# A product moved from VectorE to GpSimd and a reciprocal cut in two, in the attention of a perceiver layer

## The chip, the cores and the metric

The kernel is one program on one core of a Trainium2 chip. The metric is the device time of one execution in microseconds (us), as the median of three runs. A core has four computing engines that work side by side, each in the order of its own instructions: TensorE (PE in the rows) multiplies matrices, VectorE (DVE) and ScalarE (ACT) work on tiles in SBUF and PSUM, and GpSimd (POOL) works on tiles in SBUF. SyncE (SP) issues the transfers. The engines wait for one another through counting semaphores.

## The reference

The layer is a cross-attention of 512 tokens to 8192 context rows with 16 heads of 32 columns and a small MLP, then a local attention, then a feed-forward with quantized weights. The change touches the cross-attention alone:

```python
q = (x @ Wq + bq).reshape(B, N, NUM_HEADS, HEAD_DIM)
k = (y @ Wk + bk).reshape(B, M, NUM_HEADS, HEAD_DIM)
v = (y @ Wv + bv).reshape(B, M, NUM_HEADS, HEAD_DIM)
scores = jnp.einsum('bnhd,bmhd->bhnm', q, k) * scale
attn = jax.nn.softmax(scores, axis=-1)
out = jnp.einsum('bhnm,bmhd->bnhd', attn, v).reshape(B, N, IMAGE_DIM)
```

## The kernel before

The attention runs head by head (`h = 2 * i + s`, 16 heads), and in a head block by block: 16 blocks `q` (QUADS) of 512 keys. The softmax needs the largest score of each row before the exponentials, so two computations run interleaved. For the present head the scores are computed with the keys on the partitions (`scores`, L1120), four tiles to a block, and ScalarE takes their exponentials (L1337). For a head that comes two blocks less than one head later, the scores are computed a first time with the tokens on the partitions (`pre`, L1080), four tiles to a block, and VectorE takes the row maximum of each (`tile_max`, L1380). Those first scores stand in three PSUM banks (PRE_BANKS), so a `pre` tile can't start before the maximum of the tile three places earlier is taken. TILE_ORDER is 0, 3, 1, 2. Tile 3 (SUM_J) is read twice: after its maximum ScalarE overwrites it with exponentials and sums them (`sum_tile`, L1293). The numbers that come out of this, one for each block, are `part_sum`.

TensorE's order in a block is PE_ORDER: score 0, pre tile 0, score 1, pre tile 3, a denominator step, score 2, pre tiles 1 and 2, score 3. Behind them comes the product of the exponentials with the values (`weighted`, L1133), for the block before.

The denominators of the softmax are collected in three ways: GpSimd adds three of a block's four tiles of exponentials for 384 tokens (`add_up`, L1525 and L1529); TensorE sums the fourth (L1144) and at the end what GpSimd added (`denominator`, L1160); and for the last 128 tokens the sums come from `part_sum`. These have to be weighted first. ScalarE computes the 16 weights after block 1 (`weigh`, L1301), VectorE multiplies them with `part_sum` (L1392) and adds the 16 products (L1394) at block 3 (`take_share`), ScalarE spreads the result on a diagonal after block 3 (`spread_share`, L1308), and TensorE adds it to the denominators in block 5 (`add_share`, L1169). Each of these steps counts up `share_steps` by one.

The head before is finished inside the next one: `denominator` at the end of block 1, the reciprocal of 128 columns in PSUM by VectorE ahead of block 2's maxima (`invert`, L1398), `output` on TensorE at the end of block 5 (L1178), and `scale_out` on VectorE ahead of block 6's maxima (L1405). Nothing is scheduled at run time: all orders are those of the code. In the last head no first scores are left to compute.

Of the kernel before, what the change touches and what calls it, by code (L numbers as in the profile page):

```python
# [22 lines left out]
ALU = mybir.AluOpType  # L23
# [7 lines left out]
P = 128  # L31
# [7 lines left out]
H = 16  # L39
# [43 lines left out]
class Chain:  # L83
# [14 lines left out]
    def wait(self):  # L98
        self.eng.wait_ge(self.sem, self.n + self.moving)
# [35 lines left out]
def perceiver(nc, a, out):  # L135

    with ExitStack() as whole:
# [75 lines left out]
        part_sum = piece([2, QUADS])  # L213
        part_share = piece([QUADS])
# [35 lines left out]
        def of_block(ap, c):  # L250

            return ap.rearrange("p (j c r) -> p c j r", c=P // HD, r=HD)[:, c]
# [632 lines left out]
        with ExitStack() as st:  # L885
# [14 lines left out]
            recip = sb("recip", [P, P])  # L900
# [7 lines left out]
            den_ps = banks[:, DEN_BANK]  # L908
# [4 lines left out]
            share_steps = sem("share_steps")  # L913
# [7 lines left out]
            recip_ready = sem("recip_ready")  # L921
# [20 lines left out]
            LASTPAIR = H // 2 - 1  # L942
# [26 lines left out]
            def ahead(q, last):  # L969

                return last >= (1 if q < QUADS - AHEAD else 2)

            WEIGH_AT, SHARE_AT, SHARE_ADD_AT = 1, 3, 5
            LAST_SUMMED = QUADS - 2

            def summed_tiles(h, q):

                if not (isinstance(h, int) and h == H - 1):
                    return POOL_TILES
                return DVE_TILES if q < LAST_SUMMED else 0  # L980
# [9 lines left out]
            def quad_no(i, s, q):  # L990

                return 2 * QUADS * i + QUADS * s + q
# [82 lines left out]
            def _(pe):  # L1075
# [61 lines left out]
                def add_to_denominator(i, s, q):  # L1137

                    h = 2 * i + s
                    if q == 0:  # L1140
                        wait(pe, recip_ready, h)
                    for n in range(summed_tiles(h, q), BT):
                        for t in range(TT):
                            last = nc.tensor.matmul(den_ps[t * HD:(t + 1) * HD, 0:P - HD], ones[:],  # L1144
                                                    of_block(prob[:, q % PSLOTS, n, 0:ADDED], t),
                                                    start=q == 0 and n == summed_tiles(h, q), stop=False)
                    last.then_inc(den_added, 1)
# [24 lines left out]
                def output(i, s, bank):  # L1172

                    h = 2 * i + s
                    pe.wait_ge(recip_ready, h + 1)
                    pe.wait_ge(pv_read, h + 1)
                    for t in range(TT):
                        last = nc.tensor.matmul(pre_ps[t * HD:(t + 1) * HD, bank, 0:P], fold[:],  # L1178
                                                of_block(pv_sum[:, s], t), start=True, stop=True)
                    last.then_inc(o_ready, 1)  # L1180
# [81 lines left out]
                for m in range(EARLY_M):  # L1262
                    hidden(m, range(DK - 1, DK))
                pe.wait_ge(pv_read, H)
                pe.wait_ge(recip_ready, H)
                pe.wait_ge(o_scaled, H)
                for m in range(EARLY_M, FM):
                    hidden(m, range(DK))
                for t in range(TT):
                    pe.wait_ge(h_whole, t + 1)  # L1270
                    for k in range(FM):
# [3 lines left out]
                        for p, (sh, sw) in enumerate(PRODUCTS):  # L1275
                            last = nc.tensor.matmul(banks[:, y_bank[t]], hT_halves[:, sh, k, t * P:(t + 1) * P],
                                                    w2_halves[:, k // 2, sw, k % 2 * D:(k % 2 + 1) * D],
                                                    start=k == 0 and p == 0, stop=k == FM - 1 and p == 2)
# [97 lines left out]
            def _(dve):  # L1376
                def tile_max(s, part, j, tile, bank):

                    dve.wait_ge(pre_ready, tile + 1)
                    nc.vector.tensor_reduce(tile_low[:, s, j, part:part + 1], pre_ps[:, bank], AX.X, ALU.max,  # L1380
                                            negate=True).then_inc(pre_read, 1)

                def head_max(h, s):

                    dve.wait_ge(pre_read, TILES * h - TT * AHEAD)
                    wait(dve, row_ready, h - 1)
                    nc.vector.tensor_reduce(neg_max[:, s], tile_low[:, s], AX.X, ALU.min).then_inc(max_ready, 1)

                def take_share(h, s):

                    dve.wait_ge(share_steps, 4 * h + 1)
                    nc.vector.tensor_tensor(part_share[:], part_share[:], part_sum[:, s], ALU.mult).then_inc(share_steps, 1)  # L1392
                    dve.wait_ge(share_steps, 4 * h + 2)
                    nc.vector.tensor_reduce(share[:], part_share[:], AX.X, ALU.add).then_inc(share_steps, 1)  # L1394

                def invert(i, s):
                    dve.wait_ge(den_ready, 2 * i + s + 1)
                    nc.vector.reciprocal(recip[:], den_ps[:, 0:P]).then_inc(recip_ready, 1)  # L1398

                def scale_out(i, s, bank):  # L1400
                    h = 2 * i + s
                    dve.wait_ge(recip_ready, h + 1)
                    dve.wait_ge(o_ready, h + 1)
                    wait(dve, o_stored[s], 16 * TT * i)
                    nc.vector.tensor_tensor(o_out[:, s], pre_ps[:, bank, 0:P], recip[:], ALU.mult).then_inc(o_scaled, 1)  # L1405
# [35 lines left out]
                def out_low(k):  # L1441

                    dve.wait_ge(o_high, k + 1)
                    nc.vector.scalar_tensor_tensor(out=oT_halves[:, 1, k], in0=oT[:, k], scalar=bv[:, k:k + 1],
                                                   in1=oT_halves[:, 0, k], op0=ALU.add, op1=ALU.subtract).then_inc(o_low, 1)
# [14 lines left out]
                def head(i, s, first, last):  # L1460
                    h = 2 * i + s
                    before = (i, 0) if s else (i - 1, 1)
                    for q in range(QUADS):
                        if q == 2 and not first:
                            invert(*before)
                        if q == OUTPUT_AT + 1 and not first:
                            scale_out(*before, out_bank)
                        if q == SHARE_AT:
                            take_share(h, s)
                        if ahead(q, last):  # L1470
                            s_of, part = (1 - s, q + AHEAD) if q < QUADS - AHEAD else (s, q + AHEAD - QUADS)
                            for n, j in enumerate(TILE_ORDER):
                                tile_max(s_of, part, j, TILES * h + TT * q + n,
                                         turn_of[(q, j)] % PRE_BANKS)
                        if q == QUADS - AHEAD - 1 and last >= 1:
                            head_max(h + 1, 1 - s)
                        if last == 0:
                            if q < LAST_SUMMED:
                                sum_tiles(q)
                            if q in SPLIT_AT:  # L1480
                                split_weights(SPLIT_AT.index(q))
                            if q in O_LOW_AT:
                                out_low(O_LOW_AT.index(q))
# [5 lines left out]
                    head(i, 1, False, 2)  # L1489
                head(LASTPAIR, 0, False, 1)  # L1490
                head(LASTPAIR, 1, False, 0)
                invert(LASTPAIR, 1)
                scale_out(LASTPAIR, 1, out_bank)
                split_weights(len(SPLIT_AT))
                out_low(DK - 1)
# [18 lines left out]
            @block.gpsimd  # L1514
            def _(pool):

                def add_up(i, s, q):
                    Q = quad_no(i, s, q)
                    sums = sum_pool[:, s]
                    if q:  # L1520
                        pool.wait_ge(p_ready, BT * Q + POOL_TILES)
                    if q == 1:

                        wait(pool, den_ready, 2 * i + s - 1)
                        nc.gpsimd.tensor_tensor(sums, prob[:, 0, 0:POOL_TILES, 0:ADDED], prob[:, 1, 0:POOL_TILES, 0:ADDED],  # L1525
                                                ALU.add).then_inc(pool_summed, 2)
                    elif q > 1:
                        pool.wait_ge(pool_summed, Q)
                        nc.gpsimd.tensor_tensor(sums, sums, prob[:, q % PSLOTS, 0:POOL_TILES, 0:ADDED],  # L1529
                                                ALU.add).then_inc(pool_summed, 1)  # L1530

                for s in range(2):
                    for q in range(QUADS):
                        add_up(0, s, q)
                for i in range(1, LASTPAIR):
                    for s in range(2):
                        for q in range(QUADS):
                            add_up(i, s, q)
                for q in range(QUADS):
                    add_up(LASTPAIR, 0, q)  # L1540

        xattn.close()

# [510 lines left out]
        with ExitStack() as st:  # L2054
# [8 lines left out]
            h = sb("h", [P, 512])  # L2063
# [332 lines left out]
```

## Time and profile before

| | |
|---|---|
| median of 3 runs | 1363.45 us (1362.64 to 1365.55) |
| the profiled execution, its own time | 1362.23 us |
| its span in the trace | 1360.4 us |
| the attention, from the first scores to the last denominators | about 343 to 1093 us of the span |
| one head in the middle | 47.3 us |
| granted TensorE clock in the attention | 1.00 |

PE is busy 95% of the span, DVE 82%, ACT 72%, POOL 52%. These are averages over stages of different kinds. Inside a head all four engines are busy over 80% of the time, so what counts there is which one makes another wait, and that is read from the timeline of one head. A row of the timeline is a start in us, a duration in us, the engine, the line, what is written and read, the shape and the number of merged instructions. In square brackets stands the time for which the engine was idle before, with what ended it.

### The profile page before, as it was taken

What the parts mean: (1) busy time and instruction counts of PE and PEld (TensorE: products, weight loads), DVE (VectorE), ACT (ScalarE), POOL (GpSimd) and SP (SyncE); (2) the same over time, 40 slices, a digit from 0 to 9 for tenths busy, and PEclk for the clock granted to TensorE, in tenths of its full rate; (3) what the DMA queues carried; (4) which work ended last, traced back from release to release, by engine and by line L of the source; (5) the groups of instructions that cost most, each with busy time, mean ns of one, the idle gap of its engine ahead of it and who ended that gap; (6) DMA issues with size and microseconds to landing.
All of it is one profiled execution on the core that took longest, in us unless ns stands there. A gap on an engine that the chain in (4) does not pass through costs nothing. (4 is left out here: it accounts for less than half of the span.)

```text
span 1360.4 us, 39341 instructions
## 1 busy us (share of the span) xinstructions
PE 1297.9 (95%) x16386; PEld 665.6 (49%) x16386; DVE 1118.7 (82%) x1819; ACT 976.4 (72%) x2002; POOL 708.3 (52%) x320
## 2 busy tenths in 40 slices
PE   7999999999899999999999999999999999999998
PEld 4444444444345444544544454454444445566454
DVE  5768888888898988898888988889887745678895
ACT  4454555544899999999999999999999931354332
POOL 0321221222688878978887888888789001111121
PEclk9999999999999999999999999999999999999999
DMA  7667777876452212122211212221211030492000
GB/s 262 188 167 203 214 228 209 226 215 171 136 170 63 64 59 70 39 70 67 53 57 57 69 40 70 69 69 40 67 59 32 4 148 1 108 212 32 1 9 24
DMA packets 127798, 137.49 MB, mean 101 GB/s; under 512 B 44995, under 2 KB 108995, under 8 KB 125699
## 3 DMA queue, kind: packets, MB, share of 16 engines
q1 hardware_dynamic: 127622, 134.98, 35.2%
q8 instruction: 130, 2.13, 0.7%
q14 instruction: 46, 0.38, 0.1%
HBM read 75.70 MB, written 44.17 MB: 88 GB/s over the span
## 5 line engine op out<-in xcount | busy, mean ns | idle before, releaser
L1380 DVE TENSOR_REDUCE early<-attend_banks 128x1 f32<-128x512 f32 x952 | 590.2, 682 | 64.0 <-PE attend_banks L1080 62.6
L1529 POOL TENSOR_TENSOR early<-early,attend_prob 128x1152 f32<-128x1152 f32 x210 | 556.4, 2650 | 65.6 <-ACT attend_prob L1337 46.1
L1337 ACT ACTIVATE attend_prob<-attend_banks 128x512 f32<-128x512 f32 x1024 | 554.4, 601 | 16.5 <-PE attend_banks L1120 9.0
L1120 PE MATMUL attend_banks<-early,k_first 97*32 97x512 f16 x2560 | 265.5, 380 | 2.9 <-ACT attend_prob L1337 1.6
L1080 PE MATMUL attend_banks<-k_first,early 96*32 96x512 f16 x2272 | 215.8, 380 | 9.0 <-DVE early L1380 7.7
L1293 ACT ACTIVATE attend_banks<-attend_banks,early 128x512 f32<-128x512 f32 x238 | 160.0, 672 | 18.3 <-DVE early L1380 18.3
L1120 PE MATMUL attend_banks<-early,attend_k_rest 97*32 97x512 f16 x1536 | 162.0, 380 | 1.1 <-ACT attend_prob L1337 0.9
L1080 PE MATMUL attend_banks<-attend_k_rest,early 96*32 96x512 f16 x1536 | 143.4, 380 | 8.9 <-DVE early L1380 8.9
L1133 PE MATMUL attend_banks<-attend_prob,attend_vh_odd 128*32 128x512 f32 x1024 | 135.6, 592 | 0.0
L1133 PE MATMUL attend_banks<-attend_prob,wkv_area 128*32 128x512 f32 x1024 | 135.6, 592 | 0.0
L1080 PEld LDWEIGHTS attend_banks<-k_first,early 96*32 96x32 f16 x2272 | 74.8, 95 | 113.9 <-DVE early L1380 91.8
L513 POOL TENSOR_TENSOR project_w_whole<-project_grid,project_qscale 128x704 f32<-128x704 f32 x24 | 33.3, 1386 | 172.6 <-DVE project_grid L667 172.6
L1120 PEld LDWEIGHTS attend_banks<-early,k_first 97*32 97x32 f16 x2560 | 82.7, 95 | 47.4 <-ACT attend_prob L1337 30.3
L567 ACT ACTIVATE project_v<-project_v_ps 128x512 f32<-128x512 f32 x64 | 38.1, 597 | 84.7 <-PE project_v_ps L806 84.7
L1144 PE MATMUL attend_banks<-attend_prob,ones 128*32 128x96 f32 x2208 | 96.0, 245 | 0.0
L1144 PEld LDWEIGHTS attend_banks<-attend_prob,ones 128*32 128x32 f32 x2208 | 75.6, 110 | 34.6 <-issue 1.2
L1080 PEld LDWEIGHTS attend_banks<-attend_k_rest,early 96*32 96x32 f16 x1536 | 48.1, 95 | 81.9 <-DVE early L1380 68.8
L507 POOL TENSOR_TENSOR project_qn<-early,project_qinv 128x704 f32<-128x704 f32 x24 | 38.0, 1583 | 88.0 <-issue 50.2
L549 ACT ACTIVATE early<-project_k_ps,project_bk 128x512 f32<-128x512 f32 x64 | 44.0, 687 | 54.0 <-PE project_k_ps L787 52.0
L804 PE MATMUL project_v_ps<-project_w_hi,project_yT_hi 128*128 128x512 f16 x192 | 73.8, 384 | 5.7 <-ACT project_v L567 5.7
L787 PE MATMUL project_k_ps<-project_yT_hi,project_w_hi 128*128 128x512 f16 x192 | 72.5, 379 | 2.3 <-ACT project_q_hi L603 1.4
L805 PE MATMUL project_v_ps<-project_w_lo,project_yT_hi 128*128 128x512 f16 x192 | 73.7, 384 | 0.0
(230 smaller groups left out, 1997.0 us busy)
## 6 DMA issues: line engine op xcount, KB each, us to landing
v_scratch<-project_v SPq DMA_DIRECT2D x16, 1024.0 KB, 8.9
early<-in_ctx_dram SPq DMA_DIRECT2D x16, 768.0 KB, 6.2
k_first<-k_scratch SPq DMA_DIRECT2D x36, 256.0 KB, 3.4
k_scratch<-project_k_hi SPq DMA_DIRECT2D x64, 128.0 KB, 3.0
k_scratch<-project_k_lo SPq DMA_DIRECT2D x64, 128.0 KB, 3.1
attend_vh_odd<-v_scratch SPq DMA_DIRECT2D x8, 1024.0 KB, 5.1
wkv_area<-v_scratch SPq DMA_DIRECT2D x7, 1024.0 KB, 5.0
attend_k_rest<-k_scratch SPq DMA_DIRECT2D x24, 256.0 KB, 3.4
```

The source lines that it names most:

```text
L549: nc.scalar.activation(kf[:, g % 2], k_ps[:, g % 2], ACT.Identity, bias=bk[:, g:g + 1], scale=1.0 / WSCALE).then_inc(kf_ready, 1)
L787: last = nc.tensor.matmul(k_ps[:, g % 2], (w_lo if p == 2 else w_hi)[:, 0, k, cols], (yT_lo if p == 1 else yT_hi)[:, u, k], start=(k, p) = ...
L804: nc.tensor.matmul(v_ps[:, t % 2], yT_hi[:, u, k, cols], w_hi[:, 1, k], start=k == 0, stop=False)
L805: nc.tensor.matmul(v_ps[:, t % 2], yT_hi[:, u, k, cols], w_lo[:, 1, k], start=False, stop=False)
L1080: last = nc.tensor.matmul(pre_ps[c * HD:(c + 1) * HD, bank, :], q_stack[0:KROWS, h, queries], keys_at(s, part * BLK, (part + 1) * BLK)[0:K ...
L1120: last = nc.tensor.matmul(s_ps[c * HD:(c + 1) * HD, s_bank(h, n), :], key_rows[:, c * HD:(c + 1) * HD], q_stack[0:KROWS + 1, h, :], start= ...
L1133: last = nc.tensor.matmul(pv_ps[t * HD:(t + 1) * HD, :], vh[s][:, BT * q + t, :], prob[:, q % PSLOTS, t, :], start=q == 0, stop=q == QUADS ...
L1144: last = nc.tensor.matmul(den_ps[t * HD:(t + 1) * HD, 0:P - HD], ones[:], of_block(prob[:, q % PSLOTS, n, 0:ADDED], t), start=q == 0 and n ...
L1293: nc.scalar.activation(pre_ps[:, bank], pre_ps[:, bank], ACT.Exp, bias=tile_low[:, s, SUM_J, part:part + 1], accum_out=part_sum[:, s, part ...
L1337: nc.scalar.activation(prob[:, q % PSLOTS, t, :], s_ps[:, s_bank(h, BT * q + t)], ACT.Exp).then_inc(p_ready, 1)
L1380: nc.vector.tensor_reduce(tile_low[:, s, j, part:part + 1], pre_ps[:, bank], AX.X, ALU.max, negate=True).then_inc(pre_read, 1)
L1529: nc.gpsimd.tensor_tensor(sums, sums, prob[:, q % PSLOTS, 0:POOL_TILES, 0:ADDED], ALU.add).then_inc(pool_summed, 1)
```

## The change

`take_share` loses its multiplication. GpSimd does it (`multiply`), behind its addition for block 2, and the steps that follow move one block later: the sum of the products on VectorE to block 4, `spread_share` to the end of block 4, and `add_share` to block 6. `invert` now takes 64 of the 128 columns; the first half stands ahead of block 2's first maximum and the second half ahead of its third. `recip_ready` counts two for each head.

```diff
-            WEIGH_AT, SHARE_AT, SHARE_ADD_AT = 1, 3, 5
+            INVERT_AT = 2
+            WEIGH_AT, MULTIPLY_AT, SHARE_AT, SHARE_ADD_AT = 1, 2, 4, 6
...
                 def take_share(h, s):
 
-                    dve.wait_ge(share_steps, 4 * h + 1)
-                    nc.vector.tensor_tensor(part_share[:], part_share[:], part_sum[:, s], ALU.mult).then_inc(share_steps, 1)
                     dve.wait_ge(share_steps, 4 * h + 2)
                     nc.vector.tensor_reduce(share[:], part_share[:], AX.X, ALU.add).then_inc(share_steps, 1)
 
-                def invert(i, s):
+                def invert(i, s, half):
+
+                    cols = slice(half * P // 2, (half + 1) * P // 2)
                     dve.wait_ge(den_ready, 2 * i + s + 1)
-                    nc.vector.reciprocal(recip[:], den_ps[:, 0:P]).then_inc(recip_ready, 1)
+                    nc.vector.reciprocal(recip[:, cols], den_ps[:, cols]).then_inc(recip_ready, 1)
...
                     for q in range(QUADS):
-                        if q == 2 and not first:
-                            invert(*before)
...
+                        if not first and q == INVERT_AT and not ahead(q, last):
+                            for half in range(2):
+                                invert(*before, half)
                         if ahead(q, last):
...
                             for n, j in enumerate(TILE_ORDER):
+                                if not first and q == INVERT_AT and n % 2 == 0:
+                                    invert(*before, n // 2)
                                 tile_max(s_of, part, j, TILES * h + TT * q + n,
...
+                def multiply(h, s):
+
+                    pool.wait_ge(share_steps, 4 * h + 1)
+                    nc.gpsimd.tensor_tensor(part_share[:], part_share[:], part_sum[:, s], ALU.mult).then_inc(share_steps, 1)
+
...
                         nc.gpsimd.tensor_tensor(sums, sums, prob[:, q % PSLOTS, 0:POOL_TILES, 0:ADDED],
                                                 ALU.add).then_inc(pool_summed, 1)
+                    if q == MULTIPLY_AT:
+                        multiply(2 * i + s, s)
```

The other hunks double the value of each wait on `recip_ready`, cut the last head's reciprocal in two as well, and give GpSimd the product of the last head.

VectorE, from the last blocks of one head to the last of the next. Before: the maxima (L1380), the whole reciprocal ahead of block 2's four, then product and sum (L1392, L1394).

```order
L1380 TENSOR_REDUCE early<-attend_banks 128x1 x16
L1398 RECIPROCAL attend_recip<-attend_banks 128x128
L1380 TENSOR_REDUCE early<-attend_banks 128x1 x4
L1392 TENSOR_TENSOR early<-early 128x16
L1394 TENSOR_REDUCE early<-early 128x1
L1380 TENSOR_REDUCE early<-attend_banks 128x1 x12
L1405 TENSOR_TENSOR attend_o_out<-attend_banks,attend_recip 128x128
L1380 TENSOR_REDUCE early<-attend_banks 128x1 x32
```

The same place after the change, with lines one higher:

```order
L1381 TENSOR_REDUCE early<-attend_banks 128x1 x16
L1399 RECIPROCAL attend_recip<-attend_banks 128x64
L1381 TENSOR_REDUCE early<-attend_banks 128x1 x2
L1399 RECIPROCAL attend_recip<-attend_banks 128x64
L1381 TENSOR_REDUCE early<-attend_banks 128x1 x6
L1393 TENSOR_REDUCE early<-early 128x1
L1381 TENSOR_REDUCE early<-attend_banks 128x1 x8
L1406 TENSOR_TENSOR attend_o_out<-attend_banks,attend_recip 128x128
L1381 TENSOR_REDUCE early<-attend_banks 128x1 x32
```

Two maxima now stand between the halves of the reciprocal. The product is gone, and the sum (L1393) stands ahead of block 4's maxima, six maxima behind the second half.

ScalarE, from `weigh` (L1301) in block 1 over `spread_share` (L1308). Before:

```order
L1301 ACTIVATE early<-early 128x16
L1337 ACTIVATE attend_prob<-attend_banks 128x512 x3
L1293 ACTIVATE attend_banks,early<-attend_banks,early 128x512
L1337 ACTIVATE attend_prob<-attend_banks 128x512 x4
L1293 ACTIVATE attend_banks,early<-attend_banks,early 128x512
L1337 ACTIVATE attend_prob<-attend_banks 128x512
L1308 ACTIVATE early<-ident,early 128x128
L1337 ACTIVATE attend_prob<-attend_banks 128x512 x3
```

After the change:

```order
L1302 ACTIVATE early<-early 128x16
L1338 ACTIVATE attend_prob<-attend_banks 128x512 x3
L1294 ACTIVATE attend_banks,early<-attend_banks,early 128x512
L1338 ACTIVATE attend_prob<-attend_banks 128x512 x4
L1294 ACTIVATE attend_banks,early<-attend_banks,early 128x512
L1338 ACTIVATE attend_prob<-attend_banks 128x512 x4
L1294 ACTIVATE attend_banks,early<-attend_banks,early 128x512
L1338 ACTIVATE attend_prob<-attend_banks 128x512
L1309 ACTIVATE early<-ident,early 128x128
L1338 ACTIVATE attend_prob<-attend_banks 128x512 x3
```

`spread_share` stands one block later, one block ahead of the `sum_tile` for which TensorE's `output` waits.

## Rows read from the trace of the kernel before

**Rows 1.** Busy time by engine, one head: stretch | length, PE, PEld, DVE, ACT, POOL busy.

```profile
585.86:633.19 47.33, 46.20 (x820) 23.33 (x816) 42.46 (x69) 45.25 (x102) 39.69 (x16) 1.00 0.20 59
```

**Rows 2.** Timeline of TensorE, an ordinary block (6): start, duration in us, instruction.

```profile
601.62 0.43 PE L1080 MATMUL attend_banks<-k_first,early 96*32 96x512 f16 x4
...
602.66 0.64 PE L1080 MATMUL attend_banks<-k_first,early 96*32 96x512 f16 x8
...
604.40 0.43 PE L1080 MATMUL attend_banks<-k_first,early 96*32 96x512 f16 x4
```

**Rows 3.** Timeline of TensorE, blocks 2 and 3 of the same head.

```profile
585.61 0.41 PE L1120 MATMUL attend_banks<-early,k_first 97*32 97x512 f16 x4
...
586.70 0.40 PE L1080 MATMUL attend_banks<-k_first,early 96*32 96x512 f16 x4
587.41 0.40 PE L1080 MATMUL attend_banks<-k_first,early 96*32 96x512 f16 x4 [0.31 <-DVE early L1380]
...
588.72 0.39 PE L1120 MATMUL attend_banks<-early,k_first 97*32 97x512 f16 x4
...
590.14 0.39 PE L1080 MATMUL attend_banks<-k_first,early 96*32 96x512 f16 x4
591.31 0.40 PE L1080 MATMUL attend_banks<-k_first,early 96*32 96x512 f16 x4 [0.78 <-DVE early L1380]
...
592.62 0.39 PE L1120 MATMUL attend_banks<-early,attend_k_rest 97*32 97x512 f16 x4
```

**Rows 4.** Timeline of VectorE, the same blocks, and block 6.

```profile
585.86 0.96 DVE L1398 RECIPROCAL attend_recip<-attend_banks 128x128 f32<-128x128 f32 x1 [0.36 <-PE attend_banks L1160]
586.73 2.42 DVE L1380 TENSOR_REDUCE early<-attend_banks 128x1 f32<-128x512 f32 x4
589.06 1.39 DVE L1392 TENSOR_TENSOR early<-early 128x16 f32<-128x16 f32 x1
590.49 0.17 DVE L1394 TENSOR_REDUCE early<-early 128x1 f32<-128x16 f32 x1
590.58 2.47 DVE L1380 TENSOR_REDUCE early<-attend_banks 128x1 f32<-128x512 f32 x4
...
602.09 2.48 DVE L1380 TENSOR_REDUCE early<-attend_banks 128x1 f32<-128x512 f32 x4 [0.29 <-PE attend_banks L1080]
```

**Rows 5.** Timeline of GpSimd, its additions for blocks 2 and 3.

```profile
587.79 2.62 POOL L1529 TENSOR_TENSOR early<-early,attend_prob 128x1152 f32<-128x1152 f32 x1 [0.24 <-ACT attend_prob L1337]
591.04 2.63 POOL L1529 TENSOR_TENSOR early<-early,attend_prob 128x1152 f32<-128x1152 f32 x1 [0.62 <-ACT attend_prob L1337]
```

**Rows 6.** The product's line in all heads: duration ns min/median/max, first and last start.

```profile
L1392 DVE TENSOR_TENSOR early<-early x16: 172/1406/1879, 351.9 to 1061.6; 128x16 f32<-128x16 f32 x16
```

**Rows 7.** Timeline of TensorE, block 3 of the first head.

```profile
353.06 0.40 PE L1080 MATMUL attend_banks<-attend_k_rest,early 96*32 96x512 f16 x4
354.66 0.40 PE L1080 MATMUL attend_banks<-attend_k_rest,early 96*32 96x512 f16 x4 [1.20 <-DVE early L1380]
```

**Rows 8.** Groups by line: shape, count | busy us, mean ns | idle before.

```profile
L652 DVE RECIPROCAL project_qinv<-project_qscale 128x44 f32<-128x44 f32 x24 | 10.3, 428 | 0.8
...
L1700 POOL TENSOR_TENSOR late<-local_o_norm,late 128x128 f16<-128x128 f32 x16 | 7.2, 449 | 77.1 <-ACT late L1744 77.1
```

**Rows 9.** Timeline of TensorE, start and end of block 5.

```profile
595.39 0.39 PE L1120 MATMUL attend_banks<-early,attend_k_rest 97*32 97x512 f16 x4
595.72 0.40 PE L1080 MATMUL attend_banks<-k_first,early 96*32 96x512 f16 x4
...
597.47 1.04 PE L1133 MATMUL attend_banks<-attend_prob,attend_vh_odd 128*32 128x512 f32 x8
598.41 0.43 PE L1178 MATMUL attend_banks<-wkv_area,fold 128*32 128x128 f32 x8
```

**Rows 10.** Timeline of ScalarE, blocks 2 to 5 of the same head.

```profile
587.99 0.66 ACT L1293 ACTIVATE attend_banks<-attend_banks,early 128x512 f32<-128x512 f32 x1 [0.27 <-DVE early L1380]
...
591.89 0.66 ACT L1293 ACTIVATE attend_banks<-attend_banks,early 128x512 f32<-128x512 f32 x1 [0.93 <-DVE early L1380]
...
593.04 0.40 ACT L1308 ACTIVATE early<-ident,early 128x128 f32<-128x128 f32 x1
593.34 1.57 ACT L1337 ACTIVATE attend_prob<-attend_banks 128x512 f32<-128x512 f32 x3
```

**Rows 11.** Timelines of VectorE and GpSimd around a head's end: a small reduction beside additions.

```profile
573.90 0.22 DVE L1387 TENSOR_REDUCE early<-early 128x4 f16<-128x64 f32 x1
...
570.22 8.26 POOL L1529 TENSOR_TENSOR early<-early,attend_prob 128x1152 f32<-128x1152 f32 x3
```

More of the change, by code:

```diff
@@ L1140, in add_to_denominator @@
                     if q == 0:
-                        wait(pe, recip_ready, h)
+                        wait(pe, recip_ready, 2 * h)
                     for n in range(summed_tiles(h, q), BT):
@@ L1174, in output @@
                     h = 2 * i + s
-                    pe.wait_ge(recip_ready, h + 1)
+                    pe.wait_ge(recip_ready, 2 * (h + 1))
                     pe.wait_ge(pv_read, h + 1)
@@ L1264, in _ @@
                 pe.wait_ge(pv_read, H)
-                pe.wait_ge(recip_ready, H)
+                pe.wait_ge(recip_ready, 2 * H)
                 pe.wait_ge(o_scaled, H)
@@ L1389, in take_share @@
                 def take_share(h, s):
-                    dve.wait_ge(share_steps, 4 * h + 1)
-                    nc.vector.tensor_tensor(part_share[:], part_share[:], part_sum[:, s], ALU.mult).then_inc(share_steps, 1)
                     dve.wait_ge(share_steps, 4 * h + 2)
                     nc.vector.tensor_reduce(share[:], part_share[:], AX.X, ALU.add).then_inc(share_steps, 1)
-                def invert(i, s):
+                def invert(i, s, half):
+                    cols = slice(half * P // 2, (half + 1) * P // 2)
                     dve.wait_ge(den_ready, 2 * i + s + 1)
-                    nc.vector.reciprocal(recip[:], den_ps[:, 0:P]).then_inc(recip_ready, 1)
+                    nc.vector.reciprocal(recip[:, cols], den_ps[:, cols]).then_inc(recip_ready, 1)
                 def scale_out(i, s, bank):
                     h = 2 * i + s
-                    dve.wait_ge(recip_ready, h + 1)
+                    dve.wait_ge(recip_ready, 2 * (h + 1))
                     dve.wait_ge(o_ready, h + 1)
@@ L1491, in _ @@
                 head(LASTPAIR, 1, False, 0)
-                invert(LASTPAIR, 1)
+                for half in range(2):
+                    invert(LASTPAIR, 1, half)
                 scale_out(LASTPAIR, 1, out_bank)
@@ L1540, in _ @@
                     add_up(LASTPAIR, 0, q)
+                multiply(H - 1, 1)
         xattn.close()
```

## The prediction, as it was made before the changed kernel ran

> **What bounds the kernel now.** I read first the busy times of one head. In a stretch of 47.33 us TensorE is busy 46.20, ScalarE 45.25, VectorE 42.46 and GpSimd 39.69 [rows 1]. Four engines are near full, so shares decide nothing; the question is who leaves TensorE idle. Next is TensorE's timeline in an ordinary block. The pre tile 0 starts at 601.62 and that of the next block at 604.40, so a block takes 2.78, and pieces follow each other without a hole [rows 2]. A group of four matmuls starts about 0.22 after the one before. That is a pace that only less matrix work would change. Then the blocks in which the change sits. In block 2 a pre tile starts at 587.41 where 586.70 + 0.22 = 586.92 was due: a hole of 0.49. In block 3 one starts at 591.31 where 590.36 was due: a hole of 0.95. Both are ended by a maximum of VectorE [rows 3]. By the scores that open blocks 2, 3 and 4 (585.61, 588.72, 592.62) block 2 takes 3.11 and block 3 takes 3.90 [rows 3]. The 14 heads between the first and the last repeat this. So TensorE's order is the bound, and the work that VectorE does outside its maxima makes holes in it.
>
> VectorE's timeline tells why. In an ordinary block the first maximum starts at 602.09, 0.47 after its pre tile (601.62), runs 0.68 by the group's first piece, and ends at about 602.77. The pre tile that needs its bank starts at 602.66 + 0.22 = 602.88 [rows 2, 4]. The slack is 0.11. Four maxima take 2.33 from start to start (586.73 to 589.06), 0.58 each, and 0.68 for one alone is 2.42 less three of these [rows 4]. So VectorE has 2.78 - 2.33 = 0.45 to spare in a block, but any work ahead of a first maximum shows on TensorE after 0.11.
>
> **The product.** It starts at 589.06, takes 1.39 and ends at 590.45; GpSimd's addition for block 2 started at 587.79, took 2.62 and ended at 590.41 [rows 4, 5]. In all 16 heads the median is 1.41; the least, 0.17, is that of the last head, in which GpSimd adds nothing [rows 6]. So the product's own work is 0.17, and the rest is waiting until GpSimd's addition is over. Taking it away frees VectorE at 589.06. It was ready for block 3 then, so the whole hole of 0.95 should go, if no other work fills it. In the first head the hole is 354.66 - 353.28 = 1.38 [rows 7].
>
> A rule speaks against the move. The Trainium skill (GPSIMD Engine Reference, 3.1 Elementwise — side-by-side cycle accounting) holds that elementwise work stays on VectorE, GpSimd being about half as fast for a tensor_tensor. The row shows that here 1.39 is paid for 0.17 of work. By that rule, with work alone as the price, freeing 0.17 of an engine with 0.45 to spare gains nothing from the product; that result is the third case below.
>
> **The product on GpSimd.** No row shows 16 columns there. The nearest is 128 columns in 0.449 [rows 8], the lower end is VectorE's 0.17 [rows 6], and I take 0.3, since 16 columns are nearer to the small end. It starts after 590.41, and the next addition waited 0.62 for ScalarE until 591.04 [rows 5]. So 0.3 and even 0.45 fit into GpSimd's idle time. If that cover shrinks (ScalarE will be some 0.4 earlier) the addition for block 3 is late by at most 0.3; GpSimd is busy 39.69 of 47.33 and makes it up [rows 1]. The product waits for nobody, since `weigh` ended in block 1. Its result is there at about 590.8.
>
> **The sum of products on VectorE** (0.17, 0.09 from start to start: 590.49 to 590.58 [rows 4]) now stands ahead of block 4's maxima. There VectorE will be free at about 591.5 and the first maximum is due at 592.0 (both from the schedule below). It costs nothing while the product is there by 591.9.
>
> **The reciprocal in halves.** The whole takes 0.96, 0.87 from start to start (585.86 to 586.73) [rows 4]. Another one of 44 columns takes 0.428 [rows 8]; (0.958 - 0.428) / 84 is 6.3 ns a column, so 64 columns are 0.55, or 0.46 from start to start. The bounds are 0.48 (half of the whole) and 0.96 (the columns cost nothing). Schedule of block 2 with 0.46: the first half at 585.86, the first maximum at 586.32 instead of 586.73, done at 587.00; the pre tile due at 586.92 starts then, a hole of about 0.1 instead of 0.49. The second maximum runs 586.90 to 587.58, so ScalarE's sum starts at 587.60 and not at 587.99, where it had waited 0.27 for this maximum [rows 10]. Pre tile 0 of the next block (588.72 + 0.22) started 0.95 after that sum's start, so the new one may start at 588.55, and block 3 opens at 588.33 instead of 588.72: block 2 gives back 0.39. The second half runs in 587.48 to 587.94, the third and fourth maxima start at 587.94 and 588.52, and VectorE is free at 589.10.
>
> **Block 3** then is 2.95 long, as before without its hole (3.90 - 0.95). Its first maximum would be due at 588.55 + 0.47 = 589.02 and starts at 589.10, done at 589.78; the pre tile that needs it is due 1.64 after the block opens (590.36 - 588.72), at 589.97. So the hole stays closed, with 0.2 in hand. Block 4 opens at 591.28 with pre tile 0 at 591.50 and its first maximum at 592.0. The fourth maximum of block 3 is taken by about 591.5. Both moves together take 0.95 + 0.39 = 1.34 from a head.
>
> **What moves one block later.** `spread_share` takes 0.30 of ScalarE from start to start (593.04 to 593.34) [rows 10], behind block 3, and the next pre tile 0 comes 0.11 late (595.72, where 595.61 was due) [rows 9]. Now it stands behind block 4 and delays block 5's `sum_tile`, for which `output` waits: it already starts 0.08 late (598.41, where 597.47 + 0.86 = 598.33 was due) [rows 9]. The hole of 0.11 moves from the start of block 5 to its end. `add_share` (some 0.06 of TensorE) leaves block 5, where the wait of `output` covered it, for block 6, where nothing does. I take a loss of 0.06 for each head, with bounds of 0 and 0.30, the whole of ScalarE's step. The last head's reciprocal in two pieces ends before `output` has come and costs nothing.
>
> **The sum.** The first head has no reciprocal: 1.38. Fourteen heads (the second to the fifteenth) gain 0.95 + 0.39 - 0.06 = 1.28 each: 17.9. The last gains nothing, having no maxima. Together 19.3. TensorE is the bound before and behind these places too, and the keys' transfers wait for ScalarE's progress and move with it, so the gain goes to the end. ScalarE allows it: it is busy 45.25 in a head [rows 1], and a head would take 47.33 - 1.28 = 46.05. The profiled execution took 1362.23 (1.8 around its span of 1360.4) and would take 1342.9; it stands 1.2 below the median of 1363.45, from which the forecast is 1344.2 us.
>
> **The rivals.**
> (1) *The halves buy nothing.* If a half costs as much as the whole, block 2 keeps its hole of 0.49, the second half delays the third and fourth maxima by 0.87, block 3's first maximum starts at 589.93, is done at 590.61, and the pre tile due at 590.36 is 0.25 late. A head gains 0.95 - 0.25 - 0.06 = 0.64, the kernel 14 x 0.64 + 1.38 = 10.3: 1353.1. With the halves worth nothing and no harm it is 14 x 0.89 + 1.38 = 13.8: 1349.6. For it: no row has 64 columns. Against it: 44 columns cost less than half of 128.
> (2) *Slower: the sum of products waits in the product's place.* It starts at about 591.5, in the middle of GpSimd's addition for block 3 (590.9 to 593.5), where before it fell into a gap (590.49, between 590.41 and 591.04) [rows 4, 5]. Should it wait for that addition as the product did, block 4's first maximum starts at 593.6 and not at 592.0, and the hole is 1.6 - 0.11 = 1.5. A head loses 1.5 - 1.28 = 0.22, the first 0.1, the kernel 3.2: 1366.7. It decides once that maximum starts over 1.39 late. Against it: a reduction with SBUF input at 573.90 took 0.22 in the middle of additions that ran from 570.22 for 8.26 [rows 11]. The Trainium skill (SBUF — State Buffer, Who interferes with whom) says that tensor_reduce never contends with GpSimd on trn2, while two SBUF inputs do; the trace agrees with both halves.
> (3) *Price by work alone.* The product's removal gains nothing, since another wait holds TensorE in block 3; only block 2's part stays: 14 x 0.33 = 4.6, 1358.8. Against it: the hole's end is a maximum that starts right behind the product [rows 3, 4].
> (4) *GpSimd is late.* If the product takes as long there as an addition, 2.63, it ends at 593.1, block 4's first maximum starts at 593.25, 1.28 late, and TensorE has a hole of 1.17: a head gains 0.11, the first 0.2, the kernel 1.7: 1361.7, within what counts as the same. It costs anything from 1.5 for 16 columns on, three times what 128 columns take.
>
> **How the numbers follow.** My forecast gets 0.73, (1) gets 0.14, (3) 0.06, (2) 0.04, (4) 0.03. Every hole gone (1.38 + 14 x (0.95 + 0.49 + 0.11) = 23.1) would be 1340.4, the low end. The high end takes in most of (1): 1352. A measurement of this kernel can tell 0.2% from no change, 2.7 us. Faster by more: 0.73 + 0.14 + 0.06 = 0.93; the same 0.03; slower 0.04.
>
> **What would show it.** The heads repeat every 46.05 instead of 47.33. VectorE has no instruction of over a microsecond in heads 0 to 14 but GpSimd a small one behind its second addition. The hole in TensorE's block 3 is gone and that in block 2 is about 0.1, while `output` starts some 0.2 late. ScalarE waits for no maximum in block 3. I would be wrong if a half reciprocal took over 0.7, if L1393 took over 0.3, or if a new hole stood in blocks 3 to 6.

## The result, and the profile after

| | before | after |
|---|---|---|
| median | 1363.62 us (1362.64 to 1365.55, 4 runs) | 1344.23 us (1344.14 to 1344.73, 4 runs) |
| ratio | | 0.9857, interval 0.9843 to 0.9871 |
| span of the profiled execution | 1360.4 us | 1342.5 us |
| one head in the middle | 47.35 us | 46.03 us |
| attention, first scores to last reciprocal | 749.5 us | 730.5 us |
| from there to the end of the span | 267.4 us | 269.1 us |

The kernel is 19.4 us faster by the medians; forecast were 1344.2 us and 19.3. The changed kernel's lines are one higher in TensorE's, ScalarE's and the first of VectorE's code (`pre` is L1081, `tile_max` L1381); GpSimd's product is L1525 and its addition L1539.

The busy times of one head, in the columns of [rows 1]:

```profile
579.00:625.05 46.05, 45.95 (x820) 23.84 (x816) 41.06 (x70) 45.13 (x102) 39.95 (x17) 1.00 0.21 61
```

TensorE was idle for 1.13 of such a head by its own row before (47.33 less 46.20) and is now for 0.10. VectorE lost 1.40 of busy time and GpSimd gained 0.26, an instruction (x17 for x16) that costs 0.22.

TensorE's timeline of blocks 2 and 3, which answers to [rows 3]:

```profile
578.75 0.41 PE L1121 MATMUL attend_banks<-early,k_first 97*32 97x512 f16 x4
...
579.84 0.72 PE L1081 MATMUL attend_banks<-k_first,early 96*32 96x512 f16 x8
...
581.47 0.39 PE L1121 MATMUL attend_banks<-early,k_first 97*32 97x512 f16 x4
...
582.89 0.61 PE L1081 MATMUL attend_banks<-k_first,early 96*32 96x512 f16 x8
...
584.41 0.39 PE L1121 MATMUL attend_banks<-early,attend_k_rest 97*32 97x512 f16 x4
```

Two pre tiles in a row now merge into one line of eight matmuls. In block 3 the line takes 0.61, as where nothing waits; in block 2 it takes 0.72, so a hole of 0.11 is left there. Block 2 takes 2.72 (581.47 less 578.75; it was 3.11), block 3 takes 2.94 (it was 3.90).

VectorE, which answers to [rows 4], and GpSimd, which answers to [rows 5]:

```profile
579.00 0.56 DVE L1399 RECIPROCAL attend_recip<-attend_banks 128x64 f32<-128x64 f32 x1 [0.37 <-PE attend_banks L1161]
579.47 1.24 DVE L1381 TENSOR_REDUCE early<-attend_banks 128x1 f32<-128x512 f32 x2
580.62 0.55 DVE L1399 RECIPROCAL attend_recip<-attend_banks 128x64 f32<-128x64 f32 x1
581.09 3.61 DVE L1381 TENSOR_REDUCE early<-attend_banks 128x1 f32<-128x512 f32 x6
584.62 0.16 DVE L1393 TENSOR_REDUCE early<-early 128x1 f32<-128x16 f32 x1
585.07 2.48 DVE L1381 TENSOR_REDUCE early<-attend_banks 128x1 f32<-128x512 f32 x4 [0.30 <-PE attend_banks L1081]
```

```profile
580.93 2.65 POOL L1539 TENSOR_TENSOR early<-early,attend_prob 128x1152 f32<-128x1152 f32 x1 [0.23 <-ACT attend_prob L1338]
583.54 0.23 POOL L1525 TENSOR_TENSOR early<-early 128x16 f32<-128x16 f32 x1
583.79 5.44 POOL L1539 TENSOR_TENSOR early<-early,attend_prob 128x1152 f32<-128x1152 f32 x2
```

A half reciprocal takes 0.55 and 0.47 from start to start. The six maxima of blocks 2 and 3 run without a pause over the border of the blocks. The sum of products (584.62, 0.16) lies in the middle of two additions that run from 583.79 for 5.44, and doesn't wait for them; then VectorE waits 0.30 for TensorE. ScalarE's only idle time of over 0.1 in such a head (0.29) is the one for TensorE's `output`.

### The profile page after: what moved, and what is told of

The parts are those of the page before. It is cut to its first block and busy times, and to the rows that moved or that the text cites. A ratio compares the mean times of both kernels' runs of the same rounds, so it can differ in the third digit from the quotient of the medians.

```text
span 1342.5 us, 39357 instructions
## 1 busy us (share of the span) xinstructions
PE 1293.7 (96%) x16386; PEld 668.1 (50%) x16386; DVE 1097.2 (82%) x1819; ACT 975.0 (73%) x2002; POOL 711.2 (53%) x336
## 5 line engine op out<-in xcount | busy, mean ns | idle before, releaser
L1381 DVE TENSOR_REDUCE early<-attend_banks 128x1 f32<-128x512 f32 x952 | 589.6, 681 | 65.4 <-PE attend_banks L1081 63.9
L1539 POOL TENSOR_TENSOR early<-early,attend_prob 128x1152 f32<-128x1152 f32 x210 | 557.0, 2652 | 42.5 <-ACT attend_prob L1338 22.3
L1081 PE MATMUL attend_banks<-k_first,early 96*32 96x512 f16 x2272 | 213.8, 382 | 0.7
L1081 PE MATMUL attend_banks<-attend_k_rest,early 96*32 96x512 f16 x1536 | 141.7, 380 | 0.0
L1081 PEld LDWEIGHTS attend_banks<-k_first,early 96*32 96x32 f16 x2272 | 74.2, 95 | 101.4 <-DVE early L1381 75.7
L1081 PEld LDWEIGHTS attend_banks<-attend_k_rest,early 96*32 96x32 f16 x1536 | 48.4, 95 | 67.4 <-DVE early L1381 50.9
```

What stands on the lines that cost most here:

```text
L1081: last = nc.tensor.matmul(pre_ps[c * HD:(c + 1) * HD, bank, :], q_stack[0:KROWS, h, queries], keys_at(s, part * BLK, (part + 1) * BLK)[0:K ...
```

## The experiments

All were compared with the kernel before on the same chip. In the runs of the first four that is 1364.25 us, in those of the last three 1362.94 us. Where a hole closes is seen best in the lengths of single blocks. The table has those of one head in the middle of each profile, from TensorE's first score of a block to that of the next; the last column is how often the reciprocal comes round (median).

| | block 2 | 3 | 4 | 5 | 6 | head |
|---|---|---|---|---|---|---|
| before | 3.11 | 3.90 | 2.77 | 3.24 | 2.77 | 47.35 |
| product alone | 3.11 | 2.94 | 2.77 | 3.21 | 2.83 | 46.40 |
| halves alone | 2.72 | 4.31 | 2.77 | 3.24 | 2.77 | 47.34 |
| GpSimd waits | 3.12 | 2.94 | 2.77 | 3.17 | 2.77 | 46.29 |
| late product | 2.72 | 2.94 | 4.38 | 3.27 | 2.84 | 47.68 |
| reciprocal whole, later | 2.73 | 3.20 | 2.77 | 3.22 | 2.84 | 46.29 |
| the change | 2.72 | 2.94 | 2.77 | 3.22 | 2.84 | 46.03 |
| `spread_share` later | 2.72 | 2.94 | 2.77 | 3.09 | 2.84 | 45.90 |

### Each half of the change alone

GpSimd's product alone, on the kernel before:

```diff
-            WEIGH_AT, SHARE_AT, SHARE_ADD_AT = 1, 3, 5
+            WEIGH_AT, MULTIPLY_AT, SHARE_AT, SHARE_ADD_AT = 1, 2, 4, 6
...
-                    dve.wait_ge(share_steps, 4 * h + 1)
-                    nc.vector.tensor_tensor(part_share[:], part_share[:], part_sum[:, s], ALU.mult).then_inc(share_steps, 1)
...
+                    if q == MULTIPLY_AT:
+                        multiply(2 * i + s, s)
```

> The kernel before with the product alone on GpSimd; the reciprocal stays whole and ahead of block 2's first maximum. My theory (the product's price is its wait for GpSimd's addition): block 3's hole of 0.95 goes, block 2's of 0.49 stays, output comes some 0.1 later; a head of 46.45 instead of 47.35, 1363.6 - (14 x 0.89 + 1.4) = 1349.8 us. Rival (work alone counts): 1363.

Measured: 1349.66 us, ratio 0.9898 (0.9883 to 0.9913); a head takes 46.40. The product alone brings 0.95 of a head's 1.32, and by the table all of it in block 3. VectorE at the start of that block now waits for TensorE, not the other way round:

```profile
584.02 2.50 DVE L1380 TENSOR_REDUCE early<-attend_banks 128x1 f32<-128x512 f32 x4 [0.23 <-PE attend_banks L1080]
```

The reciprocal in halves alone, that is the changed kernel with the product back on VectorE in block 3:

```diff
-            WEIGH_AT, MULTIPLY_AT, SHARE_AT, SHARE_ADD_AT = 1, 2, 4, 6
+            WEIGH_AT, SHARE_AT, SHARE_ADD_AT = 1, 3, 5
...
                 def take_share(h, s):
 
+                    dve.wait_ge(share_steps, 4 * h + 1)
+                    nc.vector.tensor_tensor(part_share[:], part_share[:], part_sum[:, s], ALU.mult).then_inc(share_steps, 1)
```

> The changed kernel with the product back on VectorE in block 3; the reciprocal stays in halves. My theory: VectorE is free 0.4 earlier after block 2 but the product still ends with GpSimd's addition, so what the halves win in block 2 is lost again in block 3; heads of 47.3, 1363.6 to 1362.6 us. Rival (the two moves add up independently): 0.39 a head, 1358.1 us.

Measured: 1364.06 us, ratio 1.000 (0.9991 to 1.001); a head takes 47.34. The time expected was worked out from 1363.6 for the kernel before, which stands at 1364.25 here. VectorE, then GpSimd, then TensorE of this kernel (its addition is L1541):

```profile
588.42 1.22 DVE L1381 TENSOR_REDUCE early<-attend_banks 128x1 f32<-128x512 f32 x2
589.56 1.39 DVE L1393 TENSOR_TENSOR early<-early 128x16 f32<-128x16 f32 x1
```

```profile
588.27 2.64 POOL L1541 TENSOR_TENSOR early<-early,attend_prob 128x1152 f32<-128x1152 f32 x1 [0.23 <-ACT attend_prob L1338]
```

```profile
590.24 0.39 PE L1081 MATMUL attend_banks<-k_first,early 96*32 96x512 f16 x4
591.81 0.40 PE L1081 MATMUL attend_banks<-k_first,early 96*32 96x512 f16 x4 [1.18 <-DVE early L1381]
```

The product ends at 590.95, GpSimd's addition at 590.91. Block 2's hole is down to 0.10 here too, but the hole in block 3 is 591.81 - 590.46 = 1.35 where it was 0.95. What the halves win in block 2 is lost one block later, to 0.01 or 0.02, because the product's end hangs on GpSimd and not on VectorE. The halves are worth 0.37 of a head (46.40 to 46.03) only once the product's wait is gone. That was run with the move to GpSimd; with the other way to remove the wait, which comes next, the halves were not run.

### Is it the addition that the product waited for?

In the kernel before the product stays on VectorE, and GpSimd's addition for block 2 waits for it:

```diff
                     elif q > 1:
+                        if q == 2:
+                            pool.wait_ge(share_steps, 4 * (2 * i + s) + 2)
                         pool.wait_ge(pool_summed, Q)
```

> The kernel before with one wait more: GpSimd's addition for block 2 starts only when VectorE's product is done, so the product meets an idle GpSimd. My theory (VectorE waited for a running addition): the product takes 0.17, block 3's hole shrinks from 0.95 to under 0.15, GpSimd runs its additions up to 1.5 later and nobody waits for them; 1350 to 1352 us. Rival (the product itself is slow there, or GpSimd's lateness costs as much): 1363 or more.

Measured: 1348.68 us, ratio 0.9887 (0.9872 to 0.9901); a head takes 46.29. The product's line over all heads, in the columns of [rows 6], and VectorE and GpSimd around one:

```profile
L1392 DVE TENSOR_TENSOR early<-early x16: 161/165/172, 352.1 to 1045.5; 128x16 f32<-128x16 f32 x16
```

```profile
583.44 0.16 DVE L1392 TENSOR_TENSOR early<-early 128x16 f32<-128x16 f32 x1
583.64 0.17 DVE L1394 TENSOR_REDUCE early<-early 128x1 f32<-128x16 f32 x1
583.76 2.49 DVE L1380 TENSOR_REDUCE early<-attend_banks 128x1 f32<-128x512 f32 x4
```

```profile
583.74 8.21 POOL L1531 TENSOR_TENSOR early<-early,attend_prob 128x1152 f32<-128x1152 f32 x3 [1.81 <-ACT attend_prob L1337]
```

One more wait makes the kernel 15.6 us faster. The product falls from a median of 1.41 to 0.165 in all heads with nothing changed about it but what GpSimd does at the time, so its price was the running addition. GpSimd idles for 1.81 instead of 0.24 ahead of the addition and then runs three in a row (8.21); nobody waits for the delay. The row names ScalarE as the releaser; by the program it is the product, whose semaphore is new there. In the kernel before, the product ends 0.03 to 0.04 after the addition in each of the 15 heads in which there is one. The Trainium skill (SBUF — State Buffer, Who interferes with whom) has the rule that a VectorE instruction with two SBUF inputs contends with a GpSimd instruction that reads SBUF, and this run agrees (1.41 beside a running addition, 0.165 without one); by the same section a tensor_reduce doesn't, and the row at 584.62 above agrees. That it is GpSimd's reading and not its writing that blocks is the skill's statement; no run here separates the two. The result is 1.3 to 3.3 us better than expected, since no hole is left in block 3 at all, and ScalarE's `spread_share`, one block earlier here, costs 0.04 instead of 0.11.

### A late product

GpSimd's product behind its addition for block 3, all else as in the changed kernel:

```diff
-            WEIGH_AT, MULTIPLY_AT, SHARE_AT, SHARE_ADD_AT = 1, 2, 4, 6
+            WEIGH_AT, MULTIPLY_AT, SHARE_AT, SHARE_ADD_AT = 1, 3, 4, 6
```

> The changed kernel with GpSimd's product behind the addition for block 3 instead of block 2, the sum of products still ahead of block 4's maxima. My theory: the product is done some 1.6 after block 4's first maximum is due, VectorE waits in order, and TensorE gets a hole of 1.6 in each of 15 heads: about 1369 us. Rival (the sum is off the path, only its value is late): 1344.2.

Measured: 1370.75 us, ratio 1.0048 (1.0033 to 1.0063): slower than the kernel before. A head takes 47.68. VectorE and GpSimd:

```profile
597.10 0.17 DVE L1393 TENSOR_REDUCE early<-early 128x1 f32<-128x16 f32 x1 [1.96 <-POOL early L1525]
597.19 1.87 DVE L1381 TENSOR_REDUCE early<-attend_banks 128x1 f32<-128x512 f32 x3
```

```profile
594.24 2.65 POOL L1539 TENSOR_TENSOR early<-early,attend_prob 128x1152 f32<-128x1152 f32 x1 [0.22 <-ACT attend_prob L1338]
596.85 0.22 POOL L1525 TENSOR_TENSOR early<-early 128x16 f32<-128x16 f32 x1
```

VectorE stands 1.96 in front of a sum that nobody needs so soon, and the four maxima stand behind it. TensorE shows it in the same block:

```profile
596.12 0.39 PE L1081 MATMUL attend_banks<-k_first,early 96*32 96x512 f16 x4
597.93 0.40 PE L1081 MATMUL attend_banks<-k_first,early 96*32 96x512 f16 x4 [1.42 <-DVE early L1381]
```

The hole is 597.93 - 596.34 = 1.59, and a head is 47.68 - 46.03 = 1.65 longer. The time is 1.75 above what was expected; part of it is the clock: the profiled execution began its attention at half the TensorE clock (last section), and its first head took 54.3. So the fourth rival's mechanism exists. It didn't come about because GpSimd's product was ready at 583.77, 0.85 before VectorE asked for it at 584.62.

### Halving or place?

The reciprocal whole again, ahead of block 2's third maximum:

```diff
-                                if not first and q == INVERT_AT and n % 2 == 0:
-                                    invert(*before, n // 2)
+                                if not first and q == INVERT_AT and n == 2:
+                                    invert(*before, 0)
...
-                    nc.vector.reciprocal(recip[:, cols], den_ps[:, cols]).then_inc(recip_ready, 1)
+                    nc.vector.reciprocal(recip[:], den_ps[:, 0:P]).then_inc(recip_ready, 2)
```

> The changed kernel with the reciprocal whole again, but ahead of block 2's third maximum. My theory (the first half fills time in which VectorE has no tile yet, and VectorE has only 0.45 to spare in a block): VectorE idles 0.44 ahead of block 2, block 2's hole shrinks to 0.06, a new one of some 0.25 opens in block 3, 1347 us. Rival (only the place counts, not the halving): 1343.6 to 1344.2.

Measured: 1349.66 us, ratio 0.9895 (0.9879 to 0.9912); a head takes 46.29, 0.26 more than the changed kernel's. VectorE and TensorE:

```profile
580.73 1.29 DVE L1381 TENSOR_REDUCE early<-attend_banks 128x1 f32<-128x512 f32 x2 [0.79 <-PE attend_banks L1081]
581.94 0.95 DVE L1398 RECIPROCAL attend_recip<-attend_banks 128x128 f32<-128x128 f32 x1
582.80 3.01 DVE L1381 TENSOR_REDUCE early<-attend_banks 128x1 f32<-128x512 f32 x5
```

```profile
581.15 0.73 PE L1081 MATMUL attend_banks<-k_first,early 96*32 96x512 f16 x8
...
584.26 0.81 PE L1081 MATMUL attend_banks<-k_first,early 96*32 96x512 f16 x8
```

VectorE idles 0.79 ahead of block 2 (0.44 was expected), where with a half in that place it idles 0.37. The maxima of block 3 start later, and the two pre tiles there take 0.81 (the lower line at 584.26), 0.20 more than 0.61. With 0.04 on another pre tile of block 3 that is nearly the head's loss. So halving matters: the first half fills time in which VectorE has no tile. Another part of the expectation fell: block 2's hole did not shrink to 0.06. Its pair (the upper line at 581.15) takes 0.73, as in the changed kernel, though no reciprocal stands ahead of the first maximum. The 0.1 left in block 2 is therefore not the half reciprocal's. Block 2 has no denominator step, so the tile that needs the first maximum's bank is due 1.09 after pre tile 0; the maximum starts 0.45 after that tile at the earliest, takes 0.69, and the waiting tile starts 0.055 after its end, which makes 1.20. The expectation of 0.06 left out these 0.055, the time from a maximum's end to the start of the tile that waited for it; it is 0.055 or 0.056 in this kernel, the changed one and the one before. By the heads the kernel should be 14 x 0.26 = 3.6 slower than the changed one, 1348.4; it was 1.3 more than that. The profiled execution has a stretch at half the TensorE clock where no other profile has one, around 1131 of its span, 1.1 after an idle time of 1.97. From the last reciprocal to the feed-forward it takes 168.6, where the changed kernel takes about 166.9 in both profiles. That fits the missing 1.3, but the other three executions were not profiled.

### ScalarE's step in its idle time

The changed kernel with `spread_share` at the end of block 5:

```diff
-                        if q == SHARE_AT:
+                        if q == SHARE_AT + 1:
                             spread_share(h)
```

> The changed kernel with ScalarE's spread_share moved from the end of block 4 to the end of block 5, where ScalarE idles 0.38 for TensorE's output anyway. My theory (it is spread_share that makes sum_tile and so output late): output's hole shrinks from 0.23 to 0.10, heads of 45.9 instead of 46.03, 1344.2 - 14 x 0.13 = 1342.4 us. Rival (output waits for something else, or add_share in block 6 now waits for the diagonal): 1344.2 or more.

> The changed kernel once more, on the same chip as the two others: 1344.2 us by both theories. The profile is taken to see whether the 3.4 us at half the granted TensorE clock at the attention's start and in the feed-forward come again at the same places.

Measured on one chip: 1342.91 us (1342.47 to 1344.70) with this, ratio 0.9852 (0.9837 to 0.9867) to the kernel before, and 1344.76 us (1344.12 to 1346.52) for the changed kernel again, ratio 0.9865 (0.9851 to 0.9880). The intervals overlap, so by the times alone the 1.9 are not certain. By the heads they are: 45.90 against 46.03 in nearly every one. TensorE and ScalarE of the new version:

```profile
589.42 1.04 PE L1134 MATMUL attend_banks<-attend_prob,attend_vh_odd 128*32 128x512 f32 x8
590.38 0.43 PE L1179 MATMUL attend_banks<-wkv_area,fold 128*32 128x128 f32 x8
```

```profile
589.50 0.67 ACT L1294 ACTIVATE attend_banks<-attend_banks,early 128x512 f32<-128x512 f32 x1
...
590.65 0.40 ACT L1309 ACTIVATE early<-ident,early 128x128 f32<-128x128 f32 x1
591.14 0.60 ACT L1338 ACTIVATE attend_prob<-attend_banks 128x512 f32<-128x512 f32 x1
```

`output` starts 590.38 - (589.42 + 0.86) = 0.10 late, in the changed kernel 0.23 (row below). ScalarE's step lies where ScalarE waited for TensorE anyway. By its median and by its heads this is the fastest version that was run.

## Why the prediction was right

**The product.** Its price was read as waiting for GpSimd's addition, from two ends 0.04 apart. The run in which GpSimd waits shows that this is so. The hole of 0.95 is gone as a whole, and GpSimd's product took 0.222 where 0.3 was taken.

**The halves.** 0.55 was worked out from 44 and 128 columns, and 0.55 it is. Block 2 gives back 0.39, as the schedule had it; the hole left is 0.11 against about 0.1, though it isn't the half's, as the whole reciprocal further back showed. The schedule for block 3 left its first maximum 0.2 in hand, and so it was: it ended at 582.91, the tile started when due, at 583.11, and no hole opened. The slack of 0.11 in an ordinary block was counted too large: 0.055 of it pass between the maximum's end and the waiting tile's start. What the sum took as independent, 0.95 + 0.39, is not: the second term exists only with the first. For the change as a whole it made no difference.

**What moved one block later.** The rows of `output`, and of the score that opens block 7, in the changed kernel:

```profile
589.09 1.05 PE L1134 MATMUL attend_banks<-attend_prob,attend_vh_odd 128*32 128x512 f32 x8
590.18 0.43 PE L1179 MATMUL attend_banks<-wkv_area,fold 128*32 128x128 f32 x8
...
593.24 0.43 PE L1121 MATMUL attend_banks<-early,attend_k_rest 97*32 97x512 f16 x4
```

It starts 0.23 late (590.18 less 589.95), as said; that is 0.15 more than in [rows 9], against 0.11 saved at block 5's start. Blocks 4 to 6 take 593.24 - 584.41 = 8.83, where they took 8.78 (592.62 to 601.40, a pre tile's 0.22 ahead of the 601.62 in [rows 2]; counted from block 2 the block shown there is 7, not 6, and so is the last row of [rows 4]). The loss of 0.06 was 0.05, with its parts otherwise than said: block 5 got 0.02 shorter and block 6 longer by 0.07. A head gained 1.32 instead of 1.28.

**The rivals.** The first is out by the half's duration of 0.55; the second by the sum's 0.16 in the middle of additions; the third by the run with the product alone, 1349.66 us; the fourth needed a product some 1.1 later than it came (the sum has to start by 584.9 to be out of the way at 585.07), and the late product shows its price.

**The sum.** That it came out to a tenth is partly luck. By the profiled spans the gain is 17.9, not 19.3; the sum had nothing for this, and the medians hide it. The attention is 19.0 shorter: 18.1 from the 14 heads behind the first (14 x 1.29, as a few have a one-off wait) and 0.9 from the first, where 1.38 was forecast. Ahead of the attention 0.6 was won, and behind it 1.7 was lost. No step of the change lies in either place. What differs there is where stretches at half the TensorE clock fell (last section): with the clock up the first head gains 1.5, and behind the attention the changed kernel's second profile takes 267.7, against 267.4 before. By these rows the change itself is worth 18.1 + 1.5 = 19.6, against 19.3, and the clock moves single executions by more than that difference. The medians agree to a tenth because the profiled execution of before, 1362.23, was under the median of its kernel, while that of after, 1344.25, was at its own. When both kernels were run again the medians were 1362.94 and 1344.76, a gain of 18.2.

## What to carry to other kernels

When a small operation takes many times its work, look at what runs on the neighbouring engine at its start and its end. If both end together, the price is a wait, and moving the operation, or having the neighbour start a little later, takes it away. Find out how much one engine may be late before another feels it (here 0.11 us by the schedule for a first maximum, 0.05 once the time up to the waiting tile's start is counted), and cut or place extra work so that it falls into time in which that engine has nothing to do. Gains in a chain of waits don't add up by themselves: a piece made shorter ahead of a step whose end hangs on another engine is worth nothing until that wait is gone.

## What the runs showed of the hardware that was not expected

The granted TensorE clock fell to half, which is 1.2 GHz, in short stretches. TensorE was busy in them, but each began inside an idle time of TensorE or at most 1.6 us after its end. The rows give length, busy times and then the clock; the first two are of the changed kernel, at the start of the attention and in the feed-forward, and the next two are the same places in its second profile:

```profile
343.80:346.80 3.00, 3.00 (x32) 1.17 (x28) 2.42 (x5) 2.78 (x7) 0.00 (x0) 0.50 1.00 245
1255.00:1258.00 3.00, 3.00 (x11) 1.41 (x10) 2.83 (x7) 0.71 (x2) 1.16 (x1) 0.50 0.02 5
```

```profile
345.00:351.00 6.00, 5.88 (x49) 1.84 (x45) 3.83 (x6) 4.40 (x11) 2.40 (x1) 0.50 1.03 252
1242.36:1246.36 4.00, 4.00 (x12) 1.47 (x13) 3.49 (x15) 1.31 (x2) 0.00 (x0) 0.59 0.00 0
```

Both falls of the first profile came under a microsecond after TensorE took up work again:

```profile
342.81 0.40 PE L1121 MATMUL attend_banks<-early,k_first 97*32 97x512 f16 x4 [1.30 <-PEq L296]
1253.93 0.65 PE L2335 MATMUL ffn_w_ps<-ident,ffn_xq 128*128 128x128 f32 x4 [3.19 <-DVE ffn_xq L2257]
```

In the kernel before the same start of the attention had the full clock, and the one fall in the feed-forward came at its very beginning:

```profile
343.45:347.45 4.00, 3.33 (x56) 1.34 (x56) 3.13 (x6) 3.56 (x8) 0.00 (x0) 1.00 0.97 262
1259.57:1263.57 4.00, 3.97 (x11) 1.53 (x12) 3.49 (x15) 1.33 (x2) 0.00 (x0) 0.57 0.00 0
```

TensorE had been idle in two gaps of 1.5 and 1.3 us just ahead of the attention in both kernels, and in all other runs too (the first is 1.5 to 1.7), though only three of the nine profiles have a fall there. So the gaps alone don't decide it. The first head up to its reciprocal took 51.9 in the changed kernel's first profile, 53.8 in its second with the longer stretch, and 51.3 in three others (the product alone, GpSimd waiting, `spread_share` later), where the clock stayed up. Against the 52.8 of before that is 1.5, where 1.38 was forecast. The late product's first head, 54.3, had a fall of that longer kind too. The feed-forward took 100.8 in the kernel before, and 102.3 in the changed one's first profile, with the fall 14.7 behind its start. In the changed kernel's second profile the fall is back at the start, and the feed-forward takes 100.8. All nine profiles are of these two kinds: 100.8 with the fall at the start (before, halves alone, the changed kernel again), 102.0 to 102.3 with it 13 to 15 later (the other six). So this difference isn't the change's. What decides where such a stretch falls stays open. It is worth 0.6 to 2.5 us here, as much as the smallest effects above, which is why heads were compared and not only times.

A GpSimd tensor_tensor of 128x16 takes 0.222 us (median of 16, by its span in the profile) beside 0.165 for the same on VectorE when nothing is in its way.
